# Two fused attention and feed-forward layers on one core: the 16-head score limit from weight norms, and a new order of the work between two stages

## Chip, core and metric

One Trainium2 chip, one of its cores. The metric is the device time of one launch in microseconds, the median of three runs. The work is spread over TensorE (PE, with PEld its weight loads), VectorE (DVE), ScalarE (ACT), GpSimd (POOL), and SyncE (SP), which issues the DMAs.

## What is computed

Input x is 4 batches of 1024 tokens with 128 features. Two layers run over it, each as `x = x + s * g`:

```
xn = layernorm(x)
# layer 0: one-head attention over 1024 tokens, and a five-matrix ternary MLP (128 -> 512 -> 512 -> 512 -> 128)
s = attn0(xn);  g = silu(mlp0(xn));  x = x + s * g
xn = layernorm(x)
# layer 1, attention part: 8 heads of 64, softmax over heads of q.k, a scan over tokens, output layer norm
q, k, v = xn@Wq+bq, xn@Wk+bk, xn@Wv+bv
states[t] = decay*states[t-1] + (1-decay)*softmax_h(q_t.k_t/8)*v_t
s = layernorm((q*states + sigmoid(q*aug)) @ Wo + bo) * ln_scale + ln_bias
# layer 1, feed-forward part: 16-head attention (head size 8) plus a top-2-of-8 mixture of experts
qkv = xn @ W_qkv + b_qkv
att = softmax(q16 k16^T / sqrt(8)) v16
moe = sum over the top 2 gates of gate_e * (xn @ W_e + b_e)
x = x + s * silu(att + moe)
```

## The kernel before, in words

The whole program is one launch; the four batches run one after the other (`for b in range(B)` on every engine), with all orders written out by hand and semaphores between the engines (`up(signal, ...)` raises one, `wait_ge(signal.at(b, n))` waits for its n-th event of the batch). Precision is kept by splitting each fp32 operand into a high and a low fp32r part; `split3` is a product of three such matmuls, `split_head` (ScalarE) and `split_rest` (VectorE) make the parts.

A batch has a first stage (layer 0), a second stage which the change rewrites, and a loop of 67 cycles in which the 16-head attention of layer 1 runs.

The second stage, on TensorE: `mq_units(0)` makes the 16-head k and q (transposed) of the first 512 tokens, `g_transposes(1)` brings the MLP's second half to token layout, `qk_unit(0)` and `(1)` make q and k columns for the 8-head part, then comes a wait until VectorE and GpSimd have finished `residual(1)`, `block_stats(1)` and `block_normalise(1)` for tokens 512 to 1023, then `transposes(xnv, ..., 1)`, `values_unit(0)`, `mq_units(1)`, `qk_unit(2)` and, mixed with them, `stack(0)` to `stack(3)`. On ScalarE `mq_head(i)` copies the four k and q results out (`mq_hi`), on VectorE `mq_rest(i)` makes their low parts (`mq_lo`). `q_unit(u)` (ScalarE) and `product(u)` (VectorE) turn a `qk_unit` into the q*k products.

A 16-head score matmul uses 32 rows per head: 8 rows of high and low parts in three copies, and 8 rows in which k has ones (column `row24`) and q has the head's negative limit (`bias_q`), so that the exponential cannot overflow. Head group 0 (4 of the 16 heads) is stacked by TensorE (`stack`, `stacked` into `q_st`, `k_st`); groups 1 to 3 are stacked by DMA from `spl`: SP waits for `kfill_ok`, then for `mq_hi` 4, and issues 72 copies of 8 rows each in four steps:

```
for j, which, first in ((1, 0, True), (1, 1, False), (0, 0, True), (0, 1, False)):
    ...
    for g4 in range(1, NG):
        for g in range(GH):
            for r in reps:
                ...
                up(stk_in[g4 - 1], sp.dma_start(dst[to:to + HDM, g4, :], spl[at:at + HDM, 2*j + which, :]), 16)
```

The steps have 24, 12, 24 and 12 copies. The ones and limits of groups 1 to 3 are filled beforehand over all 128 rows: k by three ScalarE activations (L1029, `kfill_ok`), q by three GpSimd multiplications (L872, `qfill_ok`). The limit itself is found in each batch: VectorE takes the largest absolute value of each row of k and q (`mq_maximum`, L555), multiplies them, TensorE sums them over each head (`bnd_mm`), VectorE checks that the result is within `SAFE = 40` and makes `bias_q` (L610 to L618, `bnd_ok`). Beyond it a branch `t_maxima_b` is taken, which finds true maxima.

The loop: in cycle k_ TensorE makes the scores of four heads for 128 keys and 512 queries (`m_scores(k_)`, a quad), ScalarE takes two exponentials of 128x1024 (L1048), TensorE multiplies the exponentials of cycle k_-2 with the values (`m_values`), and one side piece of other work (table `SIDE`) follows. Quads 0 to 15 are those of group 0, quad 16, the seventeenth, is the first of group 1 and waits for `stk_in[0]`.

Nearly all matmuls are recorded at the helper line L1092. ScalarE's q copies are L996, `mq_head` is L1001, `silu_g` L971; VectorE's `product` is L540, `mq_rest` L547, `split_rest` L460, `values_in` L568, normalising L452, the residual L499 and L504, the row maxima of layer 0 L484; SP's stacking copies are L352.

## Time and profile before

| | us |
|---|---|
| median of 3 runs | 1062.44 (1061.34 to 1062.52) |
| the profiled execution | 1063.32 |
| its span | 1061.5 |
| TensorE busy | 981.9 (93%) |
| ScalarE busy | 759.2 (72%) |
| VectorE busy | 567.6 (53%) |
| GpSimd busy | 203.9 (19%) |

The span runs from the first to the last recorded instruction. Busy time is the sum over an engine's instructions; idle time of an engine costs only where another waits for its result.

### The profile page before, as it was taken

Reading aid. Unit: us, or ns where it says so; the run is one execution under the profiler, and the core shown is the slowest. Engines: PE = TensorE matmul, PEld = TensorE weight load, DVE = VectorE, ACT = ScalarE, POOL = GpSimd, SP = SyncE. Lnnn points to the kernel's source line nnn. Section 1 sums busy time; section 2 is a strip of 40 time slices with the busy share of each in tenths; the row PEclk is TensorE's granted clock in tenths of the full one; section 3 lists DMA queues with packets and bytes.
Section 4 is the critical chain, followed back from the end, with each engine's and each line's share of the span. In section 5 each row is a group of like instructions: output and inputs, shape, how many; then the busy total and the mean of one; then the engine's idle time right before and its main releaser. Section 6 shows DMA issues by size and latency. Waiting matters only on the chain.

```text
span 1061.5 us, 16258 instructions
## 1 busy us (share of the span) xinstructions
PE 981.9 (93%) x6122; PEld 547.2 (52%) x6122; DVE 567.6 (53%) x1373; ACT 759.2 (72%) x926; POOL 203.9 (19%) x144
## 2 busy tenths in 40 slices
PE   2799899999999989999999988999998998999995
PEld 1588643344378853334347874334436886333431
DVE  6835834554465663463654574455547457346352
ACT  5254489988853469997965357998895436999885
POOL 3200021432120020251230002043132001015123
PEclk9999899999999989999999999999999999999998
DMA  6000033000000013200000002300000000320000
GB/s 237 1 2 1 2 49 61 1 2 1 1 22 2 1 19 50 43 2 1 1 15 8 1 1 38 51 23 1 1 1 21 2 1 10 50 32 1 1 1 23
DMA packets 14428, 20.66 MB, mean 19 GB/s; under 512 B 2848, under 2 KB 11136, under 8 KB 14080
## 3 DMA queue, kind: packets, MB, share of 16 engines
q1 hardware_dynamic: 14336, 19.41, 8.5%
q8 instruction: 60, 0.98, 0.4%
q14 instruction: 32, 0.26, 0.1%
HBM read 7.85 MB, written 2.10 MB: 9 GB/s over the span
## 4 chain that ended last, share of the span: by engine, by line
PE 72%; DVE 9%; issue 6%; ACT 6%; SPq 4%; POOL 2%; DMA 1%; DVEq 0%; POOLq 0%; ACTq 0%
PE ps L1092 70%; SPq L352 4%; ACT big L1048 3%; PE ps L1492 1%; DVE wk L540 1%; DVE st L276 1%; POOL st L865 1%; ACT xn L1020 1%; DVE xn L452 1%; DVE wk L730 1%; DVE flags L420 1%; DVE wk L477 1%; DVE qk_max L555 1%; DVE spl L460 0%; DVE big L416 0%
## 5 line engine op out<-in xcount | busy, mean ns | idle before, releaser
L1048 ACT ACTIVATE big<-ps 128x1024 f32<-128x1024 f32 x512 | 493.9, 1034 | 50.5 <-PE ps L1092 48.5
L1092 PE MATMUL ps<-big,vaug 128*32 128x512 f32 x2048 | 272.6, 604 | 3.7 <-DVE wk L730 2.6
L1092 PE MATMUL ps<-hid 32*128 32x512 f32 x1024 | 130.5, 493 | 3.9 <-ACT big L1048 2.5
L1092 PE MATMUL ps<-hid,fw_sb 128*128 128x512 f32 x416 | 100.6, 396 | 0.0
L865 POOL TENSOR_TENSOR st<-st 128x4 f32<-128x4 f32 x16 | 16.2, 1011 | 429.4 <-DVE st L529 321.3
L967 ACT ACTIVATE wk<-ps,cols_sb 128x512 f32<-128x512 f32 x64 | 40.6, 687 | 78.3 <-PE ps L1092 74.2
L1092 PEld LDWEIGHTS ps<-hid 32*128 32x128 f32 x1024 | 49.1, 181 | 77.0 <-issue 42.0
L1092 PEld LDWEIGHTS ps<-hid,fw_sb 128*128 128x128 f32 x416 | 77.8, 189 | 17.6
L878 POOL TENSOR_TENSOR qz<-qz,wk 128x512 f32<-128x512 f32 x32 | 41.2, 1287 | 235.8 <-DVE wk L700 235.8
L1092 PEld LDWEIGHTS ps<-big,vaug 128*32 128x32 f32 x2048 | 41.0, 108 | 69.7 <-issue 41.9
L718 DVE SCALAR_TENSOR_TENSOR big<-ps,sm,big 128x128 f32<-128x128 f32 x128 | 44.3, 346 | 46.4 <-PE ps L1092 35.5
L1092 PE MATMUL ps<-wk,big 128*128 128x129 f32 x512 | 61.3, 275 | 2.4 <-ACT big L978 1.5
L1092 PEld LDWEIGHTS ps<-wk,big 128*128 128x128 f32 x512 | 60.5, 191 | 5.8 <-issue 4.1
L1092 PE MATMUL ps<-xt_hi,lw_hi 128*128 128x512 f32 x112 | 53.5, 478 | 5.9 <-DVE wk L540 5.7
L957 ACT ACTIVATE wk<-ps,cols_sb 128x512 f32<-128x512 f32 x32 | 21.9, 688 | 40.0 <-PE ps L1092 40.0
L1092 PEld LDWEIGHTS ps<-lw_hi,xt_hi 128*128 128x128 f32 x96 | 18.0, 188 | 60.5 <-DVE wk L718 33.6
L1092 PE MATMUL ps<-xt_lo,lw_hi 128*128 128x512 f32 x112 | 46.7, 430 | 2.6 <-DVE xt_lo L460 2.6
L1092 PE MATMUL ps<-xt_hi,lw_lo 128*128 128x512 f32 x112 | 47.5, 424 | 0.0
L978 ACT ACTIVATE big<-ps 128x512 f32<-128x512 f32 x64 | 36.6, 602 | 14.2 <-PE ps L1092 14.1
L1092 PEld LDWEIGHTS ps<-xt_hi,lw_hi 128*128 128x128 f32 x112 | 22.7, 203 | 46.1 <-issue 8.4
L468 DVE TENSOR_TENSOR hid<-wk,hid 128x512 fp32r<-128x512 f32 x64 | 44.3, 693 | 2.2
L687 DVE TENSOR_SCALAR wk<-ps,decay 128x512 f32<-128x512 f32 x32 | 25.9, 809 | 36.6 <-PE ps L1092 36.2
(210 smaller groups left out, 1626.7 us busy)
## 6 DMA issues: line engine op xcount, KB each, us to landing
hid<-spl SPq DMA_DIRECT2D x288, 32.0 KB
xnext<-in_x SPq DMA_DIRECT2D x4, 512.0 KB, 4.1
out<-qz SPq DMA_DIRECT2D x8, 256.0 KB, 2.3
big<-in_fw SPq DMA_DIRECT2D x1, 1877.0 KB, 9.3
wk<-in_lw SPq DMA_DIRECT2D x1, 1476.0 KB, 14.2
big<-in_fw SPq DMA_DIRECT2D x1, 939.0 KB, 11.1
cst_sb<-in_cst SPq DMA_DIRECT2D x1, 440.0 KB, 4.3
xn<-in_aw SPq DMA_DIRECT2D x1, 320.0 KB, 5.3
```

Of the source, the lines that this page charges most:

```text
L276: step(v.bn_stats(bn[:, t, :], src[:, t, :]))
L352: up(stk_in[g4 - 1], sp.dma_start(dst[to:to + HDM, g4, :].bitcast(F32), spl[at:at + HDM, 2 * j + which, :].bitcast(F32)), 16)
L468: up(hid_lo, v.tensor_tensor(hidden(buf, 1, m), src, hidden(buf, 0, m).bitcast(F32), ALU.subtract))
L687: up(v_copy, v.tensor_scalar(v1[u % 4], ps[:, SIDE_BANK, :], decay[:, KM + m:KM + m + 1], decay[:, 2 * KM + m:2 * KM + m + 1], ALU.mult, A ...
L718: ins = v.scalar_tensor_tensor(acc, src, weight, acc, ALU.mult, ALU.add)
L865: up(rstd_ok, g_.tensor_tensor(rstd[:, tl], var[:, tl], half[:, tl], ALU.pow))
L878: up(qs_ok, g_.tensor_tensor(qz[:, m, sl], qz[:, m, sl], v1[u % 4], ALU.mult))
L957: up(l1_act, a.activation(act32[n_ % 3], ps[:, L1_BANKS[c][m % 2], :], ACT.Silu, scale=col("w1s", m)))
L967: up(h_act, a.activation(act32[n_ % 3], ps[:, banks[m], :], ACT.Gelu, scale=col(name, m)))
L978: up(sc_exp, a.activation(big[:, h, jt // 2, (jt % 2) * CH:(jt % 2 + 1) * CH], ps[:, SC_BANKS[n_ % 4], :], ACT.Exp))
L1048: up(ms_exp, a.activation(prob[:, at:at + 2 * CH].rearrange("p (h n) -> p h n", n=CH), ps[:, bank:bank + 2, :], ACT.Exp, scale=HDM ** -0.5))
L1092: return t_.matmul(out_, lhsT, rhs, start=start, stop=stop, **kw)
```

## The change

1. The limit of the 16 heads is computed once, in the setup of batch 0: the norm of each weight column of k and q, times the square root of 128 (the length of a layer-normalised token), plus the absolute bias, replaces the largest value found in the data. `mq_maximum` and the per-batch limit are gone. VectorE squares the weights before the row maxima, TensorE sums them (`squares`), GpSimd takes a power; VectorE's remaining operations follow the eight row maxima; the last ones stand ahead of `mq_rest(0)` in batch 0. The branch register is loaded once.
2. TensorE: `stack(0)` and `values_unit(0)` stand ahead of the second `transposes`; `stack(1)` and `qk_unit(2)` behind them; `mq_units(1)` comes after `qk_unit(2)` and waits for `prod_ok` 2, since it writes new banks (`MQ_BANKS` has four entries, two of them those of `qk_unit(1)`).
3. VectorE: `mq_rest(0)` ahead of `residual(1)`, `mq_rest(1)` ahead of normalising, `product(1)` behind `values_in(0)`.
4. k's ones are written by four DMAs on SP (`ones_in`) into the eight rows that need them, once `w3_mm` 2 is up; ScalarE's three fills are gone. GpSimd's q fills wait for `ln_ok` 2 and the one limit.
5. ScalarE: the stackings follow the q copies more closely, and in cycles 0 and 1 of the loop the q copy stands between the two exponentials.

```diff
-QK_BANKS = ((2, 3), (4, 5), (2, 3), (4, 5), (0, 1), (6, 7), (6, 7))
-MQ_BANKS = (0, 1)
-STK_BANKS = (6, 7, 6, 6)
+QK_BANKS = ((2, 3), (4, 5), (2, 3), (0, 1), (6, 7), (6, 7), (6, 7))
+MQ_BANKS = (0, 1, 4, 5)
+STK_BANKS = (0, 1, 4, 5)
+BOUND_BANK, VALUES_BANKS = 6, (7, 7, 7)
...
+                sp.wait_ge(w3_mm.sem, w3_mm.at(b, 2))
+                for g in range(GH):
+                    rows_ = slice(QUAD * g + 3 * HDM, QUAD * (g + 1))
+                    up(ones_in, sp.dma_start(k_st[rows_, 1:NG, :].rearrange("p g (a n) -> p (g a) n", n=P).bitcast(F32),
+                                             one_row[0:HDM, :].bitcast(F32).unsqueeze(1).broadcast_to([HDM, (NG - 1) * S // P, P])), 16)
...
-                    if j == 1:
-                        sp.wait_ge(kfill_ok.sem, kfill_ok.at(b, NG - 1))
-                    else:
+                    if j == 0:
                         sp.wait_ge(qfill_ok.sem, qfill_ok.at(b, NG - 1))
...
+                if b == 0:
+                    w_ = lw_hi[:, LM:LM + 2 * D].bitcast(F32)
+                    done(v.tensor_tensor(squares, w_, w_, ALU.mult), "squares")
                 for t in range(NT):
                     row_maximum(t)
+                    if b == 0 and t == 2:
+                        v.wait_ge(setup_p, 5)
+                        done(v.tensor_scalar(norms, ps[:, 1, 0:2], float(D), 1e-30, ALU.mult, ALU.max), "norms")
+                        biases = cols_sb[:, COL["mbq"]:COL["mbq"] + 2]
+                        done(v.scalar_tensor_tensor(qk_max[:, 2:4], biases, -1.0, biases, ALU.mult, ALU.max))
+                if b == 0:
+                    v.wait_ge(norm_ok, 1)
+                    so_far()
+                    done(v.tensor_tensor(qk_max[:, 4:6], norms, qk_max[:, 4:6], ALU.mult))
+                    so_far()
+                    done(v.tensor_tensor(qk_max[:, 4:6], qk_max[:, 4:6], qk_max[:, 2:4], ALU.add))
+                    so_far()
+                    done(v.scalar_tensor_tensor(qk_max[:, 6:7], qk_max[:, 4:5], -1.002, qk_max[:, 5:6], ALU.mult, ALU.mult))
+                    so_far()
+                    done(v.tensor_scalar(sm[:, 7, 0:HM], cst_sb[:, CBM:CBM + HM], qk_max[:, 6:7], None, ALU.mult), "bound rows")
...
                 split_rest(xt_lo, xt_hi, T_BANKS[0], 0, xT_mm, 1, x_hi, x_lo)
+                if b == 0:
+                    v.wait_ge(bnd_mm, 1)
...
+                    need_max = v.value_load(iflag[0:1, 1:2], min_val=0, max_val=1)
+                mq_rest(0)
                 residual(1)
                 block_stats(1)
-                mq_rest(0)
+                mq_rest(1)
                 block_normalise(1)
-                mq_rest(1)
                 product(0, QK_BANKS[0][1])
-                product(1, QK_BANKS[1][1])
-                mq_maximum(0)
-                mq_maximum(1)
                 split_rest(xt_lo, xt_hi, T_BANKS[1], 1, xT_mm, 2, x_hi, x_lo)
                 values_in(0)
-                mq_maximum(2)
-                mq_maximum(3)
...
+                product(1, QK_BANKS[1][1])
+                product(2, QK_BANKS[2][1])
                 mq_rest(2)
-                product(2, QK_BANKS[2][1])
...
 # GpSimd
+            g_.wait_ge(setup_v, marks["norms"])
+            g_.tensor_tensor(qk_max[:, 4:6], qk_max[:, 0:2], half[:, 0:2], ALU.pow).then_inc(norm_ok, 1)
...
-                    g_.wait_ge(bnd_ok.sem, bnd_ok.at(b, 1))
+                    g_.wait_ge(bnd_ok, 1)
+                    g_.wait_ge(ln_ok.sem, ln_ok.at(b, 2))
...
 # ScalarE
                 q_unit(1, QK_BANKS[1][0])
-                for g4 in range(1, NG):
-                    a.wait_ge(w3_mm.sem, w3_mm.at(b, 2))
-                    up(kfill_ok, a.activation(k_st[:, g4, :], col("row24").broadcast_to([P, S]), ACT.Copy))
+                stacked(0)
                 split_head(xt_hi, T_BANKS[1], 1, xT_mm, 2, x_hi)
+                stacked(1)
+                q_unit(2, QK_BANKS[2][0])
                 mq_head(2)
                 mq_head(3)
-                q_unit(2, QK_BANKS[2][0])
-                stacked(0)
                 a.activation(mrow2[:, 0:1], ones[:, 0:1], ACT.Exp)
                 q_unit(3, QK_BANKS[3][0])
-                stacked(1)
                 stacked(2)
+                stacked(3)
                 q_unit(4, QK_BANKS[4][0])
-                stacked(3)
...
+                        if e_ % 2 and what == "qk":
+                            q_unit(i, QK_BANKS[i][0])
...
 # TensorE
                 g_transposes(1)
+                if b == 0:
+                    t_.wait_ge(setup_v, marks["bound rows"])
+                    mm(ps[:, BOUND_BANK, 0:HM], ones, sm[:, 7, 0:HM], True, True).then_inc(bnd_mm, 1)
                 t_.wait_ge(pv_norm.sem, pv_norm.at(b, NT))
                 qk_unit(0)
                 qk_unit(1)
+                stack(0)
+                t_.wait_ge(res_ok.sem, res_ok.at(b, 2))
+                values_unit(0)
                 t_.wait_ge(ln_ok.sem, ln_ok.at(b, 2))
                 transposes(xnv, T_BANKS[1], 1)
-                values_unit(0)
-                t_.wait_ge(mq_lo.sem, mq_lo.at(b, 2))
-                mq_units(1)
+                stack(1)
                 t_.wait_ge(prod_ok.sem, prod_ok.at(b, 1))
                 qk_unit(2)
-                stack(0)
...
                 t_.wait_ge(prod_ok.sem, prod_ok.at(b, 2))
+                mq_units(1)
+                t_.wait_ge(stk_ok.sem, stk_ok.at(b, 2))
                 qk_unit(3)
-                t_.wait_ge(bnd_ok.sem, bnd_ok.at(b, 1))
-                stack(1)
-                t_.wait_ge(stk_ok.sem, stk_ok.at(b, 1))
                 stack(2)
-                t_.wait_ge(mq_lo.sem, mq_lo.at(b, 4))
+                stack(3)
+                t_.wait_ge(mv_ok.sem, mv_ok.at(b, 1))
                 qk_unit(4)
-                t_.wait_ge(stk_ok.sem, stk_ok.at(b, 3))
-                stack(3)
...
                     if k_ == 0:
-                        t_.wait_ge(stk_ok.sem, stk_ok.at(b, 2))
+                        t_.wait_ge(prod_ok.sem, prod_ok.at(b, 3))
+                        t_.wait_ge(stk_ok.sem, stk_ok.at(b, 4))
                     elif k_ == 1:
-                        t_.wait_ge(prod_ok.sem, prod_ok.at(b, 5))
-                    elif k_ == 4:
-                        t_.wait_ge(stk_ok.sem, stk_ok.at(b, 4))
+                        t_.wait_ge(prod_ok.sem, prod_ok.at(b, 4))
                     elif k_ % (NCH * NT) == 0:
+                        if g4 == 1:
+                            t_.wait_ge(ones_in.sem, ones_in.at(b, GH * 16))
                         t_.wait_ge(stk_in[g4 - 1].sem, stk_in[g4 - 1].at(b, stk_in[g4 - 1].per))
```

## Rows read from the trace of the kernel before

**Rows 1.** The page's first line.
```profile
span 1061.5 us, 16258 instructions
```
**Rows 2.** Windows over the second stage of the four batches: busy us of each engine, clock, DMA.
```profile
116.00:141.60 25.60, 21.88 (x83) 14.89 (x81) 16.91 (x46) 15.74 (x22) 6.60 (x4) 0.80 0.12 20
372.00:397.30 25.30, 21.83 (x83) 14.87 (x81) 16.90 (x45) 15.73 (x22) 6.60 (x4) 0.80 0.12 18
627.70:650.20 22.50, 17.75 (x83) 12.36 (x81) 16.70 (x45) 15.62 (x22) 5.42 (x4) 1.00 0.10 15
880.90:903.60 22.70, 19.00 (x83) 13.14 (x81) 16.73 (x45) 15.56 (x22) 5.39 (x4) 0.92 0.10 15
```
**Rows 3.** Windows, same columns: the stretches at the lower clock.
```profile
126.68:136.92 10.24, 9.71 (x23) 5.95 (x21) 7.22 (x19) 4.70 (x7) 1.73 (x1) 0.50 0.15 24
382.68:392.92 10.24, 9.68 (x23) 5.94 (x21) 7.21 (x19) 4.70 (x7) 1.74 (x1) 0.50 0.16 24
891.26:894.68 3.42, 3.09 (x9) 1.99 (x8) 2.86 (x6) 0.32 (x1) 0.00 (x0) 0.50 0.00 0
```
**Rows 4.** Timeline of batch 2's second stage: start us, us, engine, line, operation.
```profile
629.09 0.40 PE L1092 MATMUL ps<-xt_hi,lw_hi 128*128 128x512 f32 x1
...
630.45 1.27 ACT L1001 ACTIVATE spl<-ps,cols_sb 128x512 fp32r<-128x512 f32 x2 [0.42 <-PE ps L1092]
...
631.12 0.69 DVE L499 TENSOR_TENSOR wk<-wk,ps 128x512 f32<-128x512 f32 x1 [1.72 <-PE ps L1259]
...
634.25 0.74 DVE L547 SCALAR_TENSOR_TENSOR spl<-ps,cols_sb,spl 128x512 fp32r<-128x512 f32 x1
...
636.63 0.66 PE L1112 MATMUL ps<-cst_sb,xn 128*128 128x128 f32 x4 [2.75 <-DVE xn L452]
...
637.15 1.40 DVE L540 SCALAR_TENSOR_TENSOR wk<-ps,cols_sb,qz 128x512 f32<-128x512 f32 x2
...
637.32 0.60 ACT L943 ACTIVATE xt_hi<-ps 128x512 fp32r<-128x512 f32 x1 [0.58 <-PE ps L1112]
...
639.66 0.68 DVE L460 TENSOR_TENSOR xt_lo<-ps,xt_hi 128x512 fp32r<-128x512 f32 x1
640.25 0.55 DVE L568 TENSOR_TENSOR vaug<-ps,rows_sb 128x384 f32<-128x384 f32 x1
640.39 0.73 PE L1092 MATMUL ps<-xt_lo,lw_hi 128*128 128x512 f32 x2 [1.15 <-DVE xt_lo L460]
...
640.93 1.27 ACT L1001 ACTIVATE spl<-ps,cols_sb 128x512 fp32r<-128x512 f32 x2 [3.01 <-PE ps L1092]
...
648.68 0.75 DVE L540 SCALAR_TENSOR_TENSOR wk<-ps,cols_sb,qz 128x512 f32<-128x512 f32 x1 [1.66 <-ACT qz L996]
...
649.67 0.51 PE L1092 MATMUL ps<-hid 32*128 32x512 f32 x4 [0.16 <-DVEq L629]
```
**Rows 5.** SP's stacking copies in batches 2 and 3 (timeline), and one landing (chain).
```profile
642.29 48.20 SPq L352 DMA_DIRECT2D hid<-spl  x72
...
895.72 48.79 SPq L352 DMA_DIRECT2D hid<-spl  x72
...
938.55 2.36 DMA hid<-spl
```
**Rows 6.** Seventeenth quad in batches 2 and 3, and its exponential in batch 2.
```profile
686.93 0.50 PE L1092 MATMUL ps<-hid 32*128 32x512 f32 x4
...
688.20 3.77 ACT L1048 ACTIVATE big<-ps 128x1024 f32<-128x1024 f32 x4
...
940.96 0.51 PE L1092 MATMUL ps<-hid 32*128 32x512 f32 x4 [0.41 <-DMA hid<-spl]
```
**Rows 7.** Row maxima of batch 0 (timeline); a small operation of the limit (groups).
```profile
37.36 8.07 DVE L484 TENSOR_REDUCE mx<-ps 128x1 f32<-128x1024 f32 x7 [0.67 <-PE ps L1092]
...
L615 DVE SCALAR_TENSOR_TENSOR bias_w<-ps,flags,cst_sb 128x16 f32<-128x16 f32 x4 | 0.9, 236 | 0.1
```
**Rows 8.** Timeline of TensorE in the first cycles of batch 2's loop.
```profile
653.64 0.50 PE L1092 MATMUL ps<-xt_hi,lw_hi 128*128 128x512 f32 x1 [1.43 <-DVE wk L540]
...
655.23 0.50 PE L1092 MATMUL ps<-hid 32*128 32x512 f32 x4
```

More of the change, by code:

```diff
@@ L197, in build_program @@
         gT = big[:, 0, 0, :]
+        squares = qz[:, 2, 0:2 * D]
         heads_T = sel_r[P // 2:P, 0:CH]
@@ L585, in _ @@
                 split_rest(xt_lo, xt_hi, T_BANKS[0], 0, xT_mm, 1, x_hi, x_lo)
+                if b == 0:
+                    v.wait_ge(bnd_mm, 1)
+                    limit = ps[:, BOUND_BANK, 0:HM]
+                    done(v.tensor_reduce(flags[:, 1:2], limit, AX.X, ALU.min))
+                    so_far()
+                    done(v.tensor_scalar(flags[:, 2:3], flags[:, 1:2], -SAFE * HDM ** 0.5, None, ALU.is_ge))
+                    done(v.tensor_scalar(iflag[:, 1:2], flags[:, 1:2], -SAFE * HDM ** 0.5, None, ALU.is_lt))
+                    so_far()
+                    done(v.scalar_tensor_tensor(bias_w[:, :].rearrange("p (a g) -> p a g", g=GH),
+                                                limit.rearrange("p (a g) -> p a g", g=GH), flags[:, 2:3], in_quad, ALU.mult, ALU.mult))
+                    so_far()
+                    v.tensor_reduce(bias_q[:, :], bias_w[:, :].rearrange("p (a g) -> p a g", g=GH), AX.X, ALU.add).then_inc(bnd_ok, 1)
+                    need_max = v.value_load(iflag[0:1, 1:2], min_val=0, max_val=1)
@@ L617, in _ @@
-                own()
-                up(bnd_ok, v.tensor_reduce(bias_q[:, :], bias_w[:, :].rearrange("p (a g) -> p a g", g=GH), AX.X, ALU.add))
+                product(1, QK_BANKS[1][1])
+                product(2, QK_BANKS[2][1])
+                mq_rest(2)
                 mq_rest(3)
@@ L1000, in mq_head @@
                     a.wait_ge(mq_mm.sem, mq_mm.at(b, i + 1))
-                    up(mq_hi, a.activation(spl[:, 2 * j, c * CH:(c + 1) * CH], ps[:, MQ_BANKS[i % 2], :], ACT.Identity,
+                    up(mq_hi, a.activation(spl[:, 2 * j, c * CH:(c + 1) * CH], ps[:, MQ_BANKS[i], :], ACT.Identity,
                                            bias=col(("mbq", "mbk")[j])))
@@ L1049, in _ @@
                                                 ps[:, bank:bank + 2, :], ACT.Exp, scale=HDM ** -0.5))
-                    what, i = side_piece(b, k_)
-                    if what == "qk":
-                        q_unit(i, QK_BANKS[i][0])
-                    elif what == "q":
+                    if what == "q":
                         q_unit(i, SIDE_BANK)
@@ L1171, in _ @@
                         row_scores(2 + t // 2)
+                    if b == 0 and t == 1:
+                        t_.wait_ge(setup_v, marks["squares"])
+                        mm(ps[:, 1, 0:1], squares[:, 0:D], ones[:, 0:1], True, True)
+                        mm(ps[:, 1, 1:2], squares[:, D:2 * D], ones[:, 0:1], True, True).then_inc(setup_p, 1)
                 def block_wait(n_):
@@ L1345, in _ @@
                 qk_unit(1)
+                stack(0)
+                t_.wait_ge(res_ok.sem, res_ok.at(b, 2))
+                values_unit(0)
                 t_.wait_ge(ln_ok.sem, ln_ok.at(b, 2))
                 transposes(xnv, T_BANKS[1], 1)
[L1348 to L1350 removed]
+                stack(1)
                 t_.wait_ge(prod_ok.sem, prod_ok.at(b, 1))
                 qk_unit(2)
[L1353 to L1370 removed]
+                t_.wait_ge(prod_ok.sem, prod_ok.at(b, 2))
+                mq_units(1)
+                t_.wait_ge(stk_ok.sem, stk_ok.at(b, 2))
+                qk_unit(3)
+                stack(2)
+                stack(3)
+                t_.wait_ge(mv_ok.sem, mv_ok.at(b, 1))
+                qk_unit(4)
+                if b == 0:
+                    t_.wait_ge(bnd_ok, 1)
+                    mm(ps[:, S_FIRST, 0:1], ones, ones[:, 0:1], True, True)
+                    need_max = t_.value_load(iflag[0:1, 1:2], min_val=0, max_val=1)
                 t_.br_lt(need_max, 1, on_true="t_bound_%d" % b, on_false="t_maxima_%d" % b)
@@ L1453, in _ @@
                     if what == "qk":
-                        if i == 5:
-                            t_.wait_ge(stk_ok.sem, stk_ok.at(b, 4))
-                        else:
-                            t_.wait_ge(prod_ok.sem, prod_ok.at(b, i))
+                        t_.wait_ge(prod_ok.sem, prod_ok.at(b, i))
                         qk_unit(i)
```

50 lines of the change are left out of this document (12 added, 38 removed).

## Prediction

> **What bounds the kernel now.** I read the page first: one span of 1061.5 us [rows 1], against 1063.32 us for the profiled execution and 1062.44 us for the median of the runs; my sum is made in the span and carried to the median as a difference. Then the windows over the stretch that the change rewrites, from 0.3 us ahead of the load of the Silu table for `silu_g(1)` to the first exponential of the 16 heads: 25.6, 25.3, 22.5 and 22.7 us in the four batches, with a mean granted clock of 0.80, 0.80, 1.00 and 0.92 [rows 2]. So the stretch holds some 96 of 1061 us, and its length differs by how long TensorE ran at the lower of its levels (1.2 instead of 2.4 GHz): 10.24, 10.24, 0 and 3.42 us [rows 3]. In front of each such fall lies the same stall: TensorE idles 2.75 us until VectorE has normalised the second half (at 636.63 in batch 2, where the clock held [rows 4]). The fall costs batches 0 and 1 some 3 us each.
>
> Third, the timeline of batch 2, the undisturbed one, as the model of all four [rows 4]. Fourth, the wait that is not in the stretch but is set by it. The 72 DMAs that stack the heads of groups 1 to 3 are issued on SP's queue one after the other, 48.20 us for 72 or 0.67 us each [rows 5]. They start when ScalarE has written the fourth `mq_hi` (1.36 us after 640.93 gives 642.29 [rows 4, 5]). The loop `for g4` is inside the four steps, so the last copy that group 1 needs is number 64: 63 x 0.67 = 42.2 us after the first, and it lands 2.36 us later [rows 5]. That is start + 44.5 us; in batch 3 it was 938.55 + 2.36 - 895.72 = 45.2. Group 1 begins with the seventeenth quad of scores. In batch 2 it starts at 686.93, 44.64 us after the queue's start, and in batch 3 at 940.96, where the row names the DMA as what it waited for [rows 6]. Transfers and TensorE thus arrive together today in the batches without a long fall. The exponential of that quad starts at 688.20, 1.27 us after the scores, where 0.6 would do: 0.7 us of lateness are free [rows 6].
>
> **The change, part by part**, in batch 2's times.
>
> *Limit from norms.* It takes from VectorE four maxima and the small operations behind them in each batch, and the wait of the stacking for them. Once, in batch 0, it adds a square of 128x256, two norm products, six small VectorE operations around the row maxima and a power on GpSimd. The maxima run back to back (8.07 us for seven [rows 7]), so these are on the path: small operations took up to 0.24 us [rows 7], so six are 1.4; the square fits in front of the first maximum, and some 0.1 us of slack in front of the last goes off. I take 1.3, with bounds 0.7 and 2. Then in batch 0 `mq_rest(0)` waits for the limit's product (behind `g_transposes(1)`) and five small operations and a register load: 5 x 0.2 + 0.4 for the product, about 1.5 us ahead of the residual; bounds 1 and 2. The limit itself is below the switch: with these inputs the largest of the 16 is 57.7, worked out from the weights, against 40 x 8^0.5 = 113.1, so the branch with true maxima isn't taken.
>
> *`mq_rest(0)` ahead of `residual(1)`.* The residual starts at 631.12 now. The head copy it would sit behind ends at 630.45 + 0.64 = 631.1, and the operation takes 0.74 [rows 4]; its successor starts 0.66 after it. Normalising, and the second transposes, come 0.74 us later: 636.63 becomes 637.37.
>
> *Stacking and values ahead of the transposes.* `stack(0)` and `values_unit(0)` (about 0.6 and 1.0 us of TensorE) move into the stall. With its later end the stall is 2.75 + 0.74 - 1.6 = 1.9 us. It does not vanish, and in batch 0 it is 3.4.
>
> *`mq_units(1)` behind `prod_ok` 2.* This is the costly one. VectorE does product 0 at 637.15 today, and 0.08 later in the new order, since one `mq_rest` stands in front of normalising either way and normalising is 0.74 later while the second `mq_rest` behind it is gone. ScalarE's copy of the second half's transposes moves from 637.32 to 638.06 and ends at 638.66; the rest of that split starts at 638.75 (today, behind two maxima, at 639.66), `values_in(0)` 0.6 us behind it as today, product 1 at about 640.05, done at 640.80 [rows 4]. Only then may `mq_units(1)` start. Four products at some 0.24 us (six and a gap took 1.59 [rows 8]) come ahead of its two last ones, which start at 641.8; today they start at 640.39 [rows 4]. So the fourth `mq_hi`, and with it SP's queue, is 1.4 us later: 643.7 instead of 642.29.
>
> *Ones by DMA in place of `kfill`.* Three ScalarE copies go (they ended long before SP began), four issues come, each no dearer than the 0.67 of rows 5. They start when `w3_mm` 2 comes, near 629, and are over 10 us before 643.7. Nothing; if that cover failed, at most 2.7 us per batch on the same queue. GpSimd's fills move from behind the limit to behind normalisation, needed only for SP's 37th copy, 24 us on. Nothing too.
>
> *The first scores.* ScalarE after `mq_head(3)` (643.6): table load and its use 1.4, then q copy 3, two stackings, q copy 4 at 0.6 each, so product 4 starts near 647.6 instead of 648.68 [rows 4]. The scores came 0.99 us after that start; a register load (0.3) is gone from it. First scores: 648.3 instead of 649.67, a gain of 1.4. Then the q copy between two exponentials removes about half (0.7) of the 1.43 us for which TensorE waits for product 5 at 653.64 [rows 8]: third quad at 653.1 instead of 655.23. Together 2.1 us, and TensorE would reach the seventeenth at 686.93 - 2.1 = 684.8.
>
> *What is late next.* Copy 64 lands at 643.7 + 44.5 = 688.2. TensorE stands 3.3 us in front of the seventeenth quad, in each batch. What was won ahead of it is lost there, and the exponential starts at 688.8 instead of 688.20.
>
> **The sum without clock.** Batch 2: +0.6. Batch 3, whose stretch was 0.2 longer: +0.3. Batch 1, 2.8 longer: -2.2. Batch 0, 3.1 longer: -2.5 + 1.5 + 1.3 = +0.3. Together -1.0 us.
>
> **The clock.** A stall of 2.75 us was followed by a fall in three batches of four, 23.9 us at half speed or 6.0 per batch [rows 3]. The new one is longer, and what follows is TensorE's full loop. Per batch 6.0 / 2 = 3.0 us lost, less 0.7 free and 0.5 that falls into the stall itself: 1.8, four times 7.2. Ends: 0, and 4 x (10.24 / 2 - 0.7) = 17.7. In the stretch, the stall of 1.9 may still cost the clock at times, which moves SP's start by up to 1 us: +1 in all, ends 0 and 4. Sum: -1.0 + 7.2 + 1.0 = +7.2, or 1069.6 us.
>
> The trace shows a 2.75 us stall with a fall behind it in three of four places [rows 2, 3]. The Trainium skill (TensorE: Matmul & The Clock Gate, section "Why this matters for your kernels") advises against gaps a little longer than that one, and would have let it pass, which this trace contradicts. By that rule alone the stretch would stay clean and only the 3.3 us stands cost: -1.0 + 7.2 = 1068.6; by the rows it is 1069.6.
>
> **Rivals.**
> 1. *The wait is there, the clock holds.* For: in batch 2 the clock held behind 2.75 us. Against: three of four. Time: 1062.4 - 1.0 = 1061.4, with the setup's and the stretch's bounds 1059.5 to 1064.
> 2. *Faster: no wait at the seventeenth quad.* One mechanism: SP's queue isn't later, because VectorE reaches product 1 early, or the copies issue faster than 0.67 us. Then the gain ahead is kept: batch 2 -2.1, batch 3 -2.1 - 0.3, batch 1 -2.1 - 2.8, batch 0 -2.1 - 3.1 + 2.8: -12 us, 1050.4. It decides when copy 64 lands less than 0.7 us behind TensorE, that is, with the queue starting at 641.0 rather than 643.7; halfway there and with the clock held it is 1056. Against: the order written for TensorE itself. For: the two blocks of `mq` banks no longer share, so nothing else holds `mq_units(1)`.
> 3. *The clock falls ahead, in the stretch, and not behind.* The stall of 1.9 us, 3.4 in batch 0, halves TensorE through `qk_unit(2)` to `(4)`; then both the scores and SP are later and the wait at the seventeenth shrinks under 3 us. At +1 to +2 us per batch on -1.0: 1063.5 to 1068, say 1065.5.
>
> **How the numbers follow.** The forecast 0.52, rival 1 0.18, rival 2 0.15, rival 3 0.15. Forecast 1069.6, its own range 1064.5 to 1079. Over all cases: the low tenth lies in rival 2's middle, 1056; the high tenth inside the forecast's long falls, 1077. A difference of 0.2%, 2.1 us, is about what can be told from no change. Slower takes the forecast, most of rival 3 (0.12): 0.64. Faster takes rival 2 and a part of rival 1 (0.05): 0.2. Same the rest, 0.16.
>
> **What would show it.** SP's first `hid<-spl` some 14.6 us after the first product of `mq_units(0)` (13.2 now), first scores 19.2 us after it (20.6 now); a row of TensorE at the seventeenth quad waiting some 3 us for DMA hid<-spl in every batch; clock windows at 0.50 right behind it; the row maxima of batch 0 ending over 1 us later. The prediction is wrong if that wait is under 1 us, or the clock stays at 1.00 behind it.

## The result and the profile after

| | before | after |
|---|---|---|
| median of 4 runs, us | 1062.11 (1061.34 to 1062.52) | 1096.63 (1092.04 to 1103.08) |
| profiled execution, its span, us | 1063.32, 1061.5 | 1092.04, 1090.2 |
| TensorE busy, us | 981.9 | 997.2 |
| ScalarE, VectorE busy, us | 759.2, 567.6 | 748.3, 556.5 |

The ratio is 1.032 (95% interval 1.029 to 1.035): 34.5 us slower. The forecast was 1069.6, with 1056 and 1077 as the low and the high tenth of all cases. Its direction and its mechanism are there, its size is not. The profiled execution is the fastest of the four, and what follows is read from it, so it accounts for 28.7 us of span.

First the page of the changed kernel: its span, its engines, the chain that ended last by engine, and the two groups of instructions around the 16-head scores.

```profile
span 1090.2 us, 16177 instructions
...
PE 997.2 (91%) x6114; PEld 552.9 (51%) x6114; DVE 556.5 (51%) x1337; ACT 748.3 (69%) x914; POOL 204.5 (19%) x145
...
PE 63%; SPq 15%; issue 7%; DVE 7%; ACT 5%; POOL 2%; DMA 1%; DVEq 0%; POOLq 0%; ACTq 0%
...
L1058 ACT ACTIVATE big<-ps 128x1024 f32<-128x1024 f32 x512 | 494.4, 1032 | 76.5 <-PE ps L1099 74.2
...
L1099 PE MATMUL ps<-hid 32*128 32x512 f32 x1024 | 135.7, 506 | 22.5 <-DMA hid<-spl 17.0
```

VectorE and ScalarE have 11 us less to do each, and the kernel is slower. SP's queue stands in the chain with 15% of the span (4% before), and the score group's row says why: 17.0 us of TensorE's idle time ended with DMA hid<-spl. The view of TensorE's waits gives the count (columns: us in total, times, longest):

```profile
PE ps L1099 <- DMA hid<-spl: 17.0, 4, 5.1
...
PE ps L1119 <- DVE xn L457: 7.4, 4, 2.5
...
PE ps L1099 <- DVEq L636: 4.1, 4, 1.1
```

Four waits for the copies, one in each batch, and four stalls in front of the second transposes. The last row is the wait in front of the first scores, for a branch that stands behind product 4 on VectorE's queue (DVEq).

The timeline of batch 2 after the change, to be laid beside [rows 4, 5, 6]; its first product of `mq_units(0)`, from which I count, is at 645.96.

```profile
645.96 0.40 PE L1099 MATMUL ps<-xt_hi,lw_hi 128*128 128x512 f32 x1
...
648.04 0.75 DVE L571 SCALAR_TENSOR_TENSOR spl<-ps,cols_sb,spl 128x512 fp32r<-128x512 f32 x1 [1.80 <-ACT spl L1011]
648.71 0.68 DVE L523 TENSOR_TENSOR wk<-wk,ps 128x512 f32<-128x512 f32 x1
...
654.20 1.11 PE L1119 MATMUL ps<-cst_sb,xn 128*128 128x128 f32 x4 [1.65 <-DVE xn L457]
...
657.27 0.74 DVE L564 SCALAR_TENSOR_TENSOR wk<-ps,cols_sb,qz 128x512 f32<-128x512 f32 x1
...
659.12 0.63 PE L1099 MATMUL ps<-xt_hi,lw_hi 128*128 128x512 f32 x1
...
661.01 1.27 ACT L1011 ACTIVATE spl<-ps,cols_sb 128x512 fp32r<-128x512 f32 x2 [2.25 <-PE ps L1099]
...
666.56 0.51 PE L1099 MATMUL ps<-hid 32*128 32x512 f32 x4 [1.04 <-DVEq L636]
...
706.99 0.80 PE L1099 MATMUL ps<-hid 32*128 32x512 f32 x4 [3.88 <-DMA hid<-spl]
707.72 1.93 PE L1099 MATMUL ps<-big,vaug 128*32 128x512 f32 x8
707.82 1.94 ACT L1058 ACTIVATE big<-ps 128x1024 f32<-128x1024 f32 x2 [3.55 <-PE ps L1099]
```

And SP's queue in the same batch (timeline of SP):

```profile
662.30 48.56 SPq L357 DMA_DIRECT2D hid<-spl  x72
```

The stall ahead of the transposes is 1.65 us instead of 2.75, but the four transposes behind it take 1.11 us where they took 0.66: the clock fell at 653.46, inside the stall. A product of 128x512 takes 0.63 us instead of 0.39 up to about 660. Product 1 (657.27) was thus done before `mq_units(1)` was reached, which starts at 659.12 only because `qk_unit(2)` ran slowly. The queue starts 16.34 us after the first product, the first scores come at 20.60. Then TensorE stands 3.88 us in front of the seventeenth quad; in this wait the clock falls again, for 10.24 us, and behind the wait eight products with the values take 1.93 us, where a group at full clock takes 1.07.

The windows of the falls at two places in batches 0, 2 and 3 (columns as in [rows 2]):

```profile
127.82:138.06 10.24, 7.74 (x22) 5.58 (x21) 6.06 (x19) 1.97 (x3) 6.61 (x4) 0.50 0.09 11
182.43:192.67 10.24, 7.14 (x36) 2.10 (x36) 1.29 (x4) 4.79 (x6) 2.52 (x2) 0.50 0.43 90
...
653.50:660.30 6.80, 6.10 (x15) 4.35 (x16) 4.05 (x9) 1.97 (x3) 5.60 (x3) 0.50 0.16 18
704.70:714.90 10.20, 7.91 (x36) 2.27 (x40) 2.45 (x5) 5.56 (x7) 2.53 (x2) 0.50 0.40 87
912.90:919.70 6.80, 5.96 (x15) 4.22 (x16) 4.19 (x10) 1.97 (x3) 5.60 (x3) 0.50 0.17 19
964.10:974.30 10.20, 7.80 (x36) 2.27 (x40) 2.46 (x5) 5.45 (x7) 2.54 (x2) 0.50 0.21 33
```

Each batch has two falls, where [rows 3] had one or none. Times of the four batches, in us after the batch's first product of `mq_units(0)`, worked out from the timelines:

| | before | after |
|---|---|---|
| that first product in batch 0, from the span's start | 117.41 | 119.67 |
| SP's first copy | 13.5, 13.5, 13.2, 13.5 | 19.9, 16.4, 16.3, 16.3 |
| first scores | 23.7, 23.4, 20.6, 20.9 | 24.2, 20.6, 20.6, 20.6 |
| seventeenth quad (scores start) | 60.9, 60.6, 57.8, 58.7 | 65.9, 61.3, 61.0, 61.0 |
| thirty-third quad | 95.2, 94.9, 92.1, 92.5 | 102.5, 98.2, 98.0, 97.9 |

So the 28.7 us of span are made up of 2.3 in the setup, 11.1 up to the seventeenth quads (5.0, 0.7, 3.2, 2.3), 10.9 between the seventeenth and the thirty-third (2.4, 2.6, 2.7, 3.2), and 4.4 elsewhere.

The last part holds one stall of 2.08 us in layer 0, at 592.56, for which the trace gives no releaser, with a fall of 3.4 us: from the thirty-third quad of batch 1 to the first product of batch 2 it is 3.9 us longer than in the kernel before. A stall of 1.8 to 2.4 us at that place of the code, in one of the batches and with a fall of 3.4 or 6.8 us, stands in the profiled executions of experiments 1, 2, 4 and 10 too.

### The profile page after: what moved, and what is told of

The parts are those of the page before. It is cut to its first block, busy times and chain, and to the rows that moved or that the text cites. A ratio compares the mean times of both kernels' runs of the same rounds, so it can differ in the third digit from the quotient of the medians.

```text
span 1090.2 us, 16177 instructions
## 1 busy us (share of the span) xinstructions
PE 997.2 (91%) x6114; PEld 552.9 (51%) x6114; DVE 556.5 (51%) x1337; ACT 748.3 (69%) x914; POOL 204.5 (19%) x145
## 4 chain that ended last, share of the span: by engine, by line
PE 63%; SPq 15%; issue 7%; DVE 7%; ACT 5%; POOL 2%; DMA 1%; DVEq 0%; POOLq 0%; ACTq 0%
PE ps L1099 61%; SPq L357 15%; ACT big L1058 2%; PE ps L1500 1%; DMA hid<-spl 1%; PE ps L1119 1%; POOL st L874 1%; DVE xn L457 1%; ACT spl L1011 1%; DVE st L278 1%; DVE wk L737 1%; DMA rows_sb<-in_rows 1%; DVE flags L425 1%; DVE wk L482 1%; ACT xn L1030 1%
## 5 line engine op out<-in xcount | busy, mean ns | idle before, releaser
L1099 PE MATMUL ps<-big,vaug 128*32 128x512 f32 x2048 | 280.5, 620 | 3.3 <-DVE wk L737 2.3
L1099 PE MATMUL ps<-hid 32*128 32x512 f32 x1024 | 135.7, 506 | 22.5 <-DMA hid<-spl 17.0
L1099 PEld LDWEIGHTS ps<-hid,fw_sb 128*128 128x128 f32 x416 | 77.7, 188 | 17.7
L988 ACT ACTIVATE big<-ps 128x512 f32<-128x512 f32 x64 | 36.6, 602 | 14.1 <-PE ps L1099 14.1
```

The costliest lines, as they stand in the source:

```text
L988: up(sc_exp, a.activation(big[:, h, jt // 2, (jt % 2) * CH:(jt % 2 + 1) * CH], ps[:, SC_BANKS[n_ % 4], :], ACT.Exp))
L1099: return t_.matmul(out_, lhsT, rhs, start=start, stop=stop, **kw)
```

## Experiments

In what follows, Q is SP's first copy, S the first scores, G the seventeenth quad and H the thirty-third, all in us after the batch's first product of `mq_units(0)`. Each kernel was timed beside the kernel before, in three sets (1 to 4, 5 to 8, 9 to 11) in which that kernel's median was 1061.97, 1062.89 and 1062.44 us; a difference of a microsecond between medians of different sets says nothing.

**1. The copies in the order in which they are needed.** The changed kernel; only the order of the 72 issues differs.

```diff
-                for j, which, first in ((1, 0, True), (1, 1, False), (0, 0, True), (0, 1, False)):
...
-                    for g4 in range(1, NG):
+                for g4 in range(1, NG):
+                    for j, which, first in ((1, 0, True), (1, 1, False), (0, 0, True), (0, 1, False)):
```

> The changed kernel with SP's stacking copies issued group by group (all 24 of group 1 first) instead of step by step; nothing else differs. Theory A, the copies of group 1 land late and the clock falls behind the wait: the row of TensorE waiting 3.9 us for DMA hid<-spl at the seventeenth quad is gone, the clock keeps its upper level there, the seventeenth quad starts some 57.4 us after the first product of mq_units(0) instead of 61.0, and the time falls by 4 x (3.9 + 3.9), from 1096.6 to about 1065. Rival B, the new order of the second stage and the set-up cost the time by themselves: the time stays above 1085.

Measured: 1063.66 us (1058.64 to 1065.44), ratio 1.0005 (0.998 to 1.003). No wait for a copy is left. G is 60.6, 55.8, 57.0 and 57.0. TensorE around the seventeenth quad of batch 2:

```profile
686.90 0.49 PE L1099 MATMUL ps<-sel_r,pick 16*128 16x512 f32 x1
687.18 0.51 PE L1099 MATMUL ps<-hid 32*128 32x512 f32 x4
687.62 1.07 PE L1099 MATMUL ps<-big,vaug 128*32 128x512 f32 x8
```

No wait in brackets, and the values' products at 1.07 us. The clock still falls in the stretch ahead of the loop (10.2, 3.4, 6.8 and 6.8 us), nowhere at the seventeenth quad. The copies' lateness and all that follows from it are worth 1096.63 - 1063.66 = 33 us, nearly the whole loss. That is twice the 17.0 us that TensorE waited. The rest of the change wins nothing that can be measured as long as the clock falls in the stretch.

**2. The wait stays, the clock is kept.** The changed kernel with 17 idle products in front of the wait (here and below idle products go to a bank that is overwritten next; the kernel's results do not change):

```diff
+                    if k_ == NCH * NT:
+                        t_.wait_ge(ms_exp.sem, ms_exp.at(b, 2 * k_ - 1))
+                        for _ in range(17):
+                            mm(ps[:, (GH * k_ + S_FIRST) % S_BANKS, :], lw_hi[:, LM:LM + P], xt_hi[:, 0:CH], True, True)
```

> The changed kernel with 17 idle products of 128x512 (some 4.0 us) on TensorE in front of its wait for group 1's copies; their results are written over by the scores. It leaves the wait and takes only the idleness away. Theory A with the clock: the seventeenth quad starts where it did (about 61 us after the first product of mq_units(0)), the four stretches of 10.24 us at clock 0.50 behind it vanish, and 4 x 3.9 = 15 us come back: 1081. Rival, the clock has no part and only the wait costs: 1096 or a little slower.

Measured: 1076.92 us (1073.22 to 1079.25), ratio 1.012 (1.007 to 1.017). Quad 17 comes as late as in the changed kernel (65.1, 61.4, 61.4, 61.6), but no fall stands behind it:

```profile
698.71 1.79 PE L1099 MATMUL ps<-xt_hi,lw_hi 128*128 128x512 f32 x7
700.43 0.51 PE L1099 MATMUL ps<-hid 32*128 32x512 f32 x4
700.87 1.07 PE L1099 MATMUL ps<-big,vaug 128*32 128x512 f32 x8
```

From G to H it is 33.8 us in each batch where the changed kernel takes 36.6 to 37.0. By the medians, the falls behind the wait are 1096.63 - 1076.92 = 19.7 of the 33 us, and the waits themselves 13.3. The profiled executions divide it the other way: up to H the falls cost 2.6 to 3.6 us a batch, 12.0 in four, and against experiment 1 the waits 4.0 to 5.1, 17.3 in four. Here the profiled execution is the slowest of its four and that of the changed kernel the fastest, and experiments 9 and 10 below give 11.7 for the falls. That both the waits and the falls cost is shown, and so is their sum; how it divides is known to some microseconds only, and 19.7 is probably too much for the falls.

**3. The late queue alone.** The kernel before; SP waits for product 3 as well before it issues the copies.

```diff
+                        sp.wait_ge(prod_ok.sem, prod_ok.at(b, 4))
```

> The kernel before with SP's queue waiting for product 3 as well, which is ready 4.7 us later than the fourth mq_hi in batch 2. Theory A: waits at the seventeenth quad of about 1.7, 1.9, 4.5 and 4.6 us, less 0.7 that is free, and the clock falls behind the two long ones at least: 1062 + 10 + 8 = 1080 (1072 to 1090). Rival B: under 1066, as the old order of the engines is untouched.

Measured: 1095.81 us (1092.72 to 1100.03), ratio 1.032 (1.027 to 1.038), the same as the whole change. Q is 19.5, 19.6, 18.2 and 19.3, and the wait in batch 2 reads so in the timeline:

```profile
705.24 0.69 PE L1093 MATMUL ps<-hid 32*128 32x512 f32 x4 [4.50 <-DMA hid<-spl]
```

The four waits are 5.1, 5.6, 4.5 and 4.8 us, 20.0 in all, each with a fall of 6.8 or 10.2 us behind it. A queue 5 to 6 us later, and nothing else, makes a kernel that is as slow. In the changed kernel the queue is 2.8 to 3.2 us later (6.4 in batch 0) and TensorE would be at the seventeenth quad sooner, with waits of 17.0 us in all; that the two times agree so closely is chance. The time lies above the range that I expected, as the queue was 6 us later in batches 0 and 1 and not 4.7, and they waited 5.1 and 5.6 us instead of 1.7 and 1.9. Here the transposes' stall is still 2.75 us.

**4. An earlier queue in the changed kernel.** `mq_units(1)` ahead of `qk_unit(2)`, VectorE's product 1 ahead of `split_rest`, ScalarE's `mq_head`s ahead of its q copy.

```diff
 # VectorE
+                product(1, QK_BANKS[1][1])
                 split_rest(xt_lo, xt_hi, T_BANKS[1], 1, xT_mm, 2, x_hi, x_lo)
                 values_in(0)
-                product(1, QK_BANKS[1][1])
 # ScalarE
-                q_unit(2, QK_BANKS[2][0])
                 mq_head(2)
                 mq_head(3)
+                q_unit(2, QK_BANKS[2][0])
 # TensorE
-                t_.wait_ge(prod_ok.sem, prod_ok.at(b, 1))
-                qk_unit(2)
                 t_.wait_ge(prod_ok.sem, prod_ok.at(b, 2))
                 mq_units(1)
+                qk_unit(2)
```

> The changed kernel with mq_units(1) back in front of qk_unit(2), product 1 back in front of the second split, and the head copies in front of the q copy. Theory A: SP's queue starts some 3 us earlier, the wait at the seventeenth quad shrinks from 3.9 to about 1 us, the fall behind it becomes short or goes, and the time falls to about 1075 (1068 to 1085). Rival B: within 3 us of 1096.6.

Measured: 1089.64 us (1082.4 to 1091.58), ratio 1.024 (1.017 to 1.030). Q is 17.4, 14.3, 13.8 and 13.7, and the waits shrink to 2.61, 2.30, 1.54 and 1.48 us, 7.9 instead of 17.0 in all. That is 9.1 us less of waiting, and the kernel is 7.0 faster. The falls did not shrink with the waits: behind them stand 13.7, 17.1, 13.7 and 3.4 us at half clock, 47.8 in all where the changed kernel has 41.0. Even the waits of 1.54 and 1.48 us each had a fall behind them, which began 1.5 and 1.9 us after the wait's end; in experiment 1, without a wait, there is none at this place. So the 1075 us that I expected, with short falls or none, did not come.

**5. Idle products in the kernel before.** 11 of them in front of its second transposes.

```diff
                 qk_unit(1)
+                for _ in range(11):
+                    mm(ps[:, T_BANKS[1], :], lw_hi[:, LM:LM + P], xt_hi[:, 0:CH], True, True)
```

> The kernel before with 11 idle products of 128x512 (2.6 us) on TensorE in the stall ahead of the second transposes, written over by these. It tests what the falls of the clock in the second stage cost. Theory: no stretch at clock 0.50 behind the transposes in any batch, first scores at 20.6 us after the first product of mq_units(0) in all four instead of 23.7, 23.4, 20.6 and 20.9; 1062 - 6 = 1056. Batches 0 and 1 then reach the seventeenth quad as early as batch 2, at the copies' landing. Rival: the falls cost nothing, as the stage waits for VectorE and ScalarE: 1062.

Measured: 1060.06 us (1058.47 to 1066.75, 12 runs), ratio 0.999 (0.997 to 1.001). The falls of [rows 3] are gone, S is 20.8, 20.6, 20.6 and 20.6 in place of 23.7, 23.4, 20.6 and 20.9, and the profiled span is 1056.8 instead of 1061.5. Over all runs no gain can be told from none; they differ by 8 us, and of one only is there a profile (it has a fall of 17.1 us in the setup, at 22.0, that has nothing to do with this edit and costs 0.5 us at most: batch 0's first product comes at 117.93, in the kernel before at 117.41).

**6. The copies' order in the kernel before.** The diff of experiment 1 on the kernel before.

> The kernel before with the copies issued group by group. Only batch 3 waited for them, by 0.6 us of which 0.7 were free: no difference, 1062 within 2 us. If the issue order itself sped anything else up, it would show here as more than 0.3%.

Measured: 1060.72 us (1058.95 to 1065.38), ratio 0.997 (0.996 to 0.999). In the kernel before transfers and TensorE arrived together [rows 6], so there was little to win: some 2.8 us by the ratio.

**7. The changed kernel with the copies' order and a clean clock in the stretch.** Experiment 1 and 7 idle products ahead of the second transposes.

```diff
+                if b == 0:
+                    t_.wait_ge(bnd_ok, 1)
+                for _ in range(7):
+                    mm(ps[:, T_BANKS[1], :], lw_hi[:, LM:LM + P], xt_hi[:, 0:CH], True, True)
```

> The changed kernel with the copies group by group and 7 idle products (1.65 us) ahead of the second transposes. Theory: the falls behind the transposes go, batches 1 to 3 reach their first scores after about 19.3 us (as batch 1 of the run with the copies' order alone did with a short fall) instead of 20.65, batch 0 after 22; 1063.7 - 1.2 x 3 - 2 = 1058. Rival: another wait of 1 to 2 us holds the first scores (the branch of VectorE behind product 4), then 1062.

Measured: 1053.58 us (1051.07 to 1057.56), ratio 0.990 (0.987 to 0.993). The lines of batch 2 show the filled stall and transposes at full clock:

```profile
635.91 1.83 PE L1099 MATMUL ps<-xt_hi,lw_hi 128*128 128x512 f32 x7
637.73 0.66 PE L1119 MATMUL ps<-cst_sb,xn 128*128 128x128 f32 x4
```

Q is 14.4, S 18.7 and G 55.0 in batches 1 to 3 alike. My prediction had 14.6, 19.2 and, for TensorE without the wait, 684.8 - 629.09 = 55.7. Its gate for the queue is there as well, `mq_units(1)` waiting for VectorE's product 1:

```profile
641.13 0.50 PE L1099 MATMUL ps<-xt_hi,lw_hi 128*128 128x512 f32 x1 [0.51 <-DVE wk L564]
```

Batch 0 is not clean. There Q, S and G are 17.8, 22.1 and 58.4, and a fall of 3.4 us is left, as in experiments 9 and 10: ahead of the idle products TensorE has stalled for 1.05 us, for `mq_rest(0)`, which stands behind VectorE's register load. In experiment 8 stall and fall are gone together. The profiled execution is the longest of the four (1057.56). Its batch 0 comes to `mq_units(0)` 4.4 to 5.4 us later than in the other profiles of the changed kernels (124.39 against 119.0 to 120.0), since its 128x512 products of the setup take 0.63 us each until 50 us from the span's start, where the others have them at 0.4 from 37 to 40 on. So the setup alone can make an execution some 5 us longer.

**8. The register load out of the way as well.** Experiment 7, with VectorE's register load in batch 0 (it reads the flag of the limit) moved from ahead of `mq_rest(0)` to just before the branch that uses it.

```diff
                 if b == 0:
...
-                    need_max = v.value_load(iflag[0:1, 1:2], min_val=0, max_val=1)
                 mq_rest(0)
...
+                if b == 0:
+                    need_max = v.value_load(iflag[0:1, 1:2], min_val=0, max_val=1)
                 v.br_lt(need_max, 1, on_true="v_bound_%d" % b, on_false="v_maxima_%d" % b)
```

> As the run before, and VectorE's load of the branch register in batch 0 stands behind product 4 instead of ahead of mq_rest(0). In the changed kernel VectorE stood still for 2.2 us behind the limit's last operation there. Theory: batch 0 gains 2 us more: 1056. Rival: the load was waited for by nobody who mattered: 1058.

Measured: 1050.85 us (1049.62 to 1051.25, 6 runs), ratio 0.988 (0.986 to 0.990): the fastest kernel of this study, 1.2% under the kernel before. VectorE in batch 0, the changed kernel first, then this one:

```profile
122.56 0.17 DVE L614 TENSOR_REDUCE bias_q<-bias_w 128x4 f32<-128x16 f32 x1
124.93 0.75 DVE L571 SCALAR_TENSOR_TENSOR spl<-ps,cols_sb,spl 128x512 fp32r<-128x512 f32 x1 [2.20 <-issue]
```

```profile
122.06 0.17 DVE L614 TENSOR_REDUCE bias_q<-bias_w 128x4 f32<-128x16 f32 x1
122.14 0.74 DVE L571 SCALAR_TENSOR_TENSOR spl<-ps,cols_sb,spl 128x512 fp32r<-128x512 f32 x1
```

The 2.20 us for which VectorE waited for nothing that the profile shows were the register load: they are gone from this place, and with them batch 0's last fall. The load is not free where it stands now. The first scores of batch 0 wait 1.83 us for VectorE's queue, 1.04 to 1.06 in the other batches:

```profile
139.63 0.51 PE L1100 MATMUL ps<-hid 32*128 32x512 f32 x4 [1.83 <-DVEq L637]
```

So Q is 2.5 us earlier in batch 0 (15.3 instead of 17.8) but S only 1.6 (20.5 instead of 22.1), and G 1.6 too. The 2.7 between the medians holds 1.1 more than this, within what four runs spread over 6 us can tell.

**9. A clean stretch, the copies' order left as the change has it.** The diff of experiment 7 on the changed kernel, without that of experiment 1.

> The changed kernel with 7 idle products of TensorE ahead of the second transposes (their results are overwritten, so nothing of the computation changes), and the copies in their written order of steps. Theory (queue start and landing are one mechanism, the clock another): the clock holds in the stretch, SP's first copy comes 14.4 us after the first product of mq_units(0) instead of 16.3, first scores at 18.7; copy 64 still lands some 44.7 us after the queue's start, near 59.1, while TensorE is at the seventeenth quad near 55.0, so the wait is about 4.1 us in every batch, the clock falls behind each, and the time is 1085 to 1092 us. Rival (the wait is a product of the fall in the stretch): with the stretch clean the wait is under 2 us and the time is under 1070.

Measured: 1085.51 us (1082.06 to 1092.18), ratio 1.024 (1.019 to 1.028). Q is 14.41 in batches 1 to 3, G 59.4, 59.1 and 59.0. The wait is 4.28, 4.16, 3.90 and 3.77 us in the four batches, here that of batch 2:

```profile
701.61 0.51 PE L1099 MATMUL ps<-hid 32*128 32x512 f32 x4 [3.90 <-DMA hid<-spl]
702.05 1.81 PE L1099 MATMUL ps<-big,vaug 128*32 128x512 f32 x8
```

with falls of 17.1, 10.2, 6.8 and 6.8 us behind. An undisturbed stretch does not take the wait away: TensorE comes 1.9 us earlier, and so do the copies. The rival, that the wait is made by the fall in the stretch, is out.

**10. Idle products at both places.** Experiments 9 and 2 together: the wait with the clock kept at both places (but for a fall of 3.4 us in batch 0's stretch).

> The same, and 17 idle products in front of the wait of the seventeenth quad as well, so that TensorE has no stall of note at either place. The wait is there, the clock is not lost. Theory: the copies land at 59.1 after the first product of mq_units(0), where the kernel with reordered copies and the same 7 products is at 55.0: 4 x 4.1 = 16 us above its 1053.6, less a little because its batch 0 fell once: 1066 to 1070 us. The recorded sum without clock said 1061.4. Rival (the wait costs less than its length because ScalarE's exponentials catch up behind it): 1056 to 1062.

Measured: 1073.85 us (1073.41 to 1076.49), ratio 1.012 (1.010 to 1.014), above the 1066 to 1070 that I expected. In the profile H is 96.9, 93.1, 93.1 and 93.1, against 92.7, 89.2, 89.3 and 89.3 in experiment 7: 4.2 + 3.9 + 3.8 + 3.8 = 15.8 us, as the theory has it. The rest of the 20.3 between the medians is not seen at these places. This execution has a stall of 2.38 us in layer 0 of batch 1, again without a releaser, with a fall of 6.8 us; from batch 0's thirty-third quad to batch 1's first product it takes 166.3 us, and 161.2 and 161.4 from batch to batch behind it. Against experiment 9 the falls behind the waits cost 1085.51 - 1073.85 = 11.7 us.

**11. The kernel before with both cures.** Experiment 6 and experiment 5 together.

> The kernel before with both: the copies issued group by group, and 11 idle products ahead of its second transposes. It tells what the change's own order of the stretch is worth once the copies no longer wait: the changed kernel with these two took 1053.6. Theory: first scores at 20.6 after the first product of mq_units(0) and 57.8 at the seventeenth quad, against 18.7 and 55.0: 4 x 2 to 2.8 us more, less 2.3 of setup and 2 of the register load: 1057 to 1060. Rival (the new order is worth nothing, the copies and the products are all of the gain): 1053 to 1055.

Measured: 1059.14 us (1058.13 to 1060.42), ratio 0.997 (0.996 to 0.998). Q 13.2, S 20.6 and G 57.8 to 57.9 in batches 1 to 3; the changed kernel with the same cures has 14.4, 18.7 and 55.0 and takes 1053.58. So the order that the change gives the second stage wins 2.8 us in each of batches 1 to 3 once its copies are not late and the clock holds; in batch 0, which has the limit, its register load and a fall of 3.4 us, it wins nothing (G is 58.3 and 58.4), and the whole is worth 5.6 us by the medians.

## Why the prediction missed

Right, by its own steps: what is late next is copy 64. The wait is in front of the seventeenth quad in each batch, by DMA hid<-spl, with a fall of the clock behind it. The model of the stretch without a fall holds to 0.7 us (experiment 7), its gate included. The landing was put at the queue's start + 44.5 us; where the clock was clean (experiment 9) quad 17 starts 44.6 to 45.1 after it. Ones by DMA and GpSimd's later fills cost nothing that shows: the four issues on SP take 5.1 us, 1.3 each rather than 0.67 at most, and end 11.0 us before the first copy (646.15 + 5.14 against 662.30).

The sum had three terms, and each can be set beside a difference of medians:

| term of the sum | forecast, us | measured, us | between |
|---|---|---|---|
| sum without clock | -1.0 | +11.7 | kernel before, experiment 10 |
| the clock behind the wait | +7.2 | +11.7 | experiments 10, 9 |
| the clock in the stretch | +1.0 | +11.1 | experiment 9, changed kernel |
| together | +7.2 | +34.5 | |

All three were too small. Each median is of four runs, so the terms are good to a few microseconds. The steps that failed:

- *The clock, in the stretch: "+1 in all, ends 0 and 4".* This is the step that made rival 3 an alternative to the forecast. Both happened, in every batch: in batches 1 to 3 a stall of 1.65 us came with 6.8 us at half speed. In batch 0 it was 10.2 us, which began at 127.80, ahead of the stall of 2.50 (128.59 to 131.09) and behind two shorter ones, 1.06 us for `mq_rest(0)` and 0.59. SP's queue then starts 16.3 us after the first product and not 14.6 (14.4 without the fall, experiment 9), and the first scores are at 20.6, where they were before, not at 19.2. The wait did not shrink, since TensorE and the copies were delayed alike. Experiment 1 against 7 prices these falls at 10 us by the medians (1063.66 against 1053.58), much as the table does; up to G the profiles show 6.9 and 8.2 us of it.
- *The clock behind the wait: 1.8 us per batch, 7.2.* I charged half of 6.0 us at half speed, an average of batches with and without a fall. Each of the four waits came with 10.2 us. From the seventeenth quad to the thirty-third the kernel takes 10.9 us more than before, experiments 9 and 10 give 11.7, and the medians of experiment 2 19.7. That is above the 7.2 by each measure, and by most of them inside its upper end of 17.7.
- *"The sum without clock": -1.0.* Its wait of 3.3 us was 4.1 in a clean stretch (55.0 for TensorE and not 55.7, and a landing at 59.1), and 3.9 to 5.1 as run. The -1.0 also contains 3 us apiece of clock that batches 0 and 1 of the kernel before had lost and that I counted as won back; in the changed kernel they fell again. Experiment 10, which keeps the clock at both places but for 3.4 us in batch 0, measures 1073.85 where the sum said 1061.4. Of these 12 us its profile shows 10: some 5 are the stall and fall in layer 0, 1.0 the setup, and up to the thirty-third quads batch 0 is 2.7 us later than the sum had it (register load, below) and batches 1 to 3 are 0.5, 0.4 and 0.3 later, all that the longer waits cost, as TensorE came 0.7 us sooner to them. The rest is open.
- *Limit from norms: +1.3.* It is 2.3. The square alone puts the first row maximum 0.68 us later (38.04 instead of the 37.36 of [rows 7]), for it did not fit in front; and after the last maximum four small operations, a memset and 0.26 us of issue take 1.0. VectorE's timeline:

```profile
37.51 0.42 DVE L494 TENSOR_TENSOR qz<-lw_hi 128x256 f32<-128x256 f32 x1
38.04 3.49 DVE L489 TENSOR_REDUCE mx<-ps 128x1 f32<-128x1024 f32 x3
...
46.79 1.23 DVE L489 TENSOR_REDUCE mx<-ps 128x1 f32<-128x1024 f32 x1 [0.17 <-PE ps L1099]
47.93 0.15 DVE L505 TENSOR_TENSOR qk_max<-qk_max 128x2 f32<-128x2 f32 x1
...
49.02 0.75 DVE L482 SCALAR_TENSOR_TENSOR wk<-ps,cols_sb,wk 128x512 f32<-128x512 f32 x1 [0.26 <-issue]
```

- *The register load in batch 0*, for which 5 x 0.2 + 0.4 leaves 0.1 of "about 1.5 us": 2.2. Moving it gave 1.6 us in batch 0's profile and 2.7 by the medians of 7 and 8. The instruction is not recorded, and its time only shows as idle time under "issue".

Against rival 2: it needed a queue that is not later, and it was later. Its size did not hold for the case it described either: experiment 1 is the kernel without the wait, and it takes 1063.66 us where 1050.4 was worked out, as the clock still falls in the stretch. Only with idle products against that as well does the change come near, 1053.58 and, with the register load moved, 1050.85.

Left open: why the other three runs of the changed kernel are 4 to 11 us longer than the profiled one. One of them (1103.08) had a mean clock of 0.949 instead of 0.963, so probably more falls; the other two had 0.963 and 0.966, so that falls of the clock alone do not tell. None of the three has a profile. A setup like that of experiment 7's profile is a candidate, not shown. What the stall in layer 0 is stays open too.

## What to carry to other kernels

When DMAs are issued one by one on a queue, the order of issue is a schedule: put first what the first consumer needs, and work out the landing of its last copy as a number beside the consumer's own time. Here swapping two loops was worth 33 us: it took a reordering of the other engines from a loss of 34 us to none. A gain of 1% came only with the clock held as well.

A stall of TensorE is to be priced with the fall that may follow it, at each place where it stands and not as an average over batches: here waits of 17 us cost some 33. A shorter stall is not by itself a harmless one; in batches 1 to 3 seven idle products in it were enough to keep the clock, while in batch 0 an earlier stall that they did not fill still cost a fall.
